# Token order, 2 KB stores, late bias product and a new order of work in a fused window-attention and top-2 expert kernel

## The reference

```
x = x + conv(ln_c(x))             # window attention on channel-normalised x
t = tokens(x)                     # (4, 16384, 64)
t = t + ffn(ln_t(t))              # top-2 of 8 experts
x = from_tokens(t)

conv: qkv = xh @ w_qkv.T;  windows of 8 x 8 tokens, 4 heads of 16
      attn = softmax(q k^T * 0.25 + bias[rel_index]);  out = (attn v) @ w_proj.T + b_proj
ffn:  p = softmax(x @ router_w + router_b);  top_p, top_i = top_k(p, 2);  top_p /= sum(top_p)
      out = sum over the two of top_p * (x @ expert_w[top_i] + expert_b[top_i])
```

## Time and profile before

| | |
|---|---|
| median of 3 runs | 1326.42 us (1312.49 to 1327.78) |
| profiled execution, own time | 1318.76 us |
| its span, first to last instruction | 1316.9 us |
| mean granted TensorE clock in it | 0.93 of full speed |
| busy share: TensorE, VectorE, ScalarE, GpSimd | 85%, 71%, 57%, 32% |
| DMA queues' share of 16 engines | 64.0% (the program's own queue) |
| DMA packets, and those under 512 B | 143202, 81984 |

### The profile page before, as it was taken

One profiled execution on the slowest core, in us unless ns is written; L12 is line 12 of the kernel. 1 busy time (PEld: TensorE's weight loads), 2 busy tenths in 40 slices (PEclk: granted clock), 3 DMA queues, 4 the chain that ended last, 5 costly groups with the idle time before them and its releaser, 6 DMA issues.

```text
span 1316.9 us, 40785 instructions
## 1 busy us (share of the span) xinstructions
PE 1124.7 (85%) x16486; PEld 600.8 (46%) x16486; DVE 938.3 (71%) x1431; ACT 753.4 (57%) x1185; POOL 417.4 (32%) x359
## 2 busy tenths in 40 slices
PE   3687998998899879988998989999899999988853
PEld 2344554445455434444444445455444544544411
DVE  3346778788777867777688777777767678778742
ACT  1366656566666655665566656666555566665410
POOL 1002233233332332333233233332333333323342
PEclk9988889898998988999899989998888899998877
DMA  4013567777666678766567875666678667656777
GB/s 158 1 29 87 138 156 183 183 177 172 145 166 147 166 166 189 165 155 154 130 164 179 189 188 139 161 162 153 152 182 189 154 162 171 159 136 141 170 174 166
DMA packets 143202, 202.75 MB, mean 154 GB/s; under 512 B 81984, under 2 KB 94656, under 8 KB 142912
## 3 DMA queue, kind: packets, MB, share of 16 engines
q1 hardware_dynamic: 143040, 200.28, 64.0%
HBM read 160.37 MB, written 23.07 MB: 139 GB/s over the span
## 4 chain that ended last, share of the span: by engine, by line
PE 37%; issue 23%; DMA 13%; POOL 10%; SPq 6%; DVE 5%; ACT 4%; POOLq 0%; ACTq 0%; DVEq 0%
DMA gz<-gates_dram 11%; PE bank L593 8%; POOL gz L903 6%; PE bank L476 6%; PE bank L509 5%; SPq L320 4%; PE bank L437 3%; PE bank L491 3%; PE bank L526 3%; POOL tt L877 2%; PE bank L533 2%; DMA gates_dram<-gsb 2%; SPq L312 2%; PE bank L464 2%; PE bank L428 1%
## 5 line engine op out<-in xcount | busy, mean ns | idle before, releaser
L1021 DVE TENSOR_TENSOR gz<-gz,tt 128x1024 f32<-128x1024 f32 x160 | 242.2, 1515 | 156.7 <-DMA gz<-gates_dram 156.7
L903 POOL TENSOR_TENSOR gz<-gz,tt 128x1024 f32<-128x1024 f32 x96 | 229.5, 2391 | 224.4 <-DMA gz<-gates_dram 224.4
L593 PE MATMUL bank<-gz,wex 64*64 64x512 f32 x2048 | 259.6, 623 | 26.4 <-issue 24.2
L877 POOL TENSOR_TENSOR tt<-prj,xs 128x512 f32<-128x512 f32 x64 | 103.6, 1639 | 361.9 <-ACT prj L764 361.9
L1000 DVE TENSOR_REDUCE mx<-bank 128x16 f32<-128x1024 f32 x128 | 156.5, 1223 | 71.9 <-PE bank L476 69.1
L476 PE MATMUL bank<-km,qs 32*64 32x128 f32 x4096 | 183.7, 297 | 0.3
L509 PE MATMUL bank<-cst,probs 128*128 128x128 f32 x1024 | 174.6, 296 | 3.2 <-ACT pt L747 3.1
L747 ACT ACTIVATE pt<-bank 128x512 f32<-128x512 f32 x256 | 152.1, 594 | 40.8 <-PE bank L509 37.7
L1007 DVE TENSOR_TENSOR probs<-bank,mx 128x1024 f32<-128x1024 f32 x128 | 156.8, 1225 | 11.5
L476 PEld LDWEIGHTS bank<-km,qs 32*64 32x64 f32 x4096 | 117.7, 140 | 92.9 <-issue 88.8
L740 ACT ACTIVATE probs<-probs 128x1024 f32<-128x1024 f32 x128 | 134.9, 1054 | 17.8 <-DVE probs L1007 17.5
(11 more groups left out here) (100 smaller groups left out, 1447.2 us busy)
## 6 DMA issues: line engine op xcount, KB each, us to landing
gz<-gates_dram SPq DMA_DIRECT2D x512, 256.0 KB, 6.8
xs<-in_x SPq DMA_DIRECT2D x32, 512.0 KB, 6.9
tx<-tt SPq DMA_DIRECT2D x128, 128.0 KB, 2.6
out<-ob SPq DMA_DIRECT2D x128, 128.0 KB, 6.8
gates_dram<-gsb SPq DMA_DIRECT2D x32, 192.0 KB, 2.1
grow<-gates_dram SPq DMA_DIRECT2D x192, 32.0 KB
gz<-in_rel SPq DMA_DIRECT2D x1, 2048.0 KB, 9.0
cst<-in_consts SPq DMA_DIRECT2D x1, 359.0 KB, 3.0
```

The costliest lines, as they stand in the source:

```text
L593: last = mm(bank[64 * x:64 * x + 64, Y_BANK + a, :], wex[64 * a:64 * a + 64, e, :], gz[64 * a:64 * a + 64, e, x * CH:(x + 1) * CH], start= ...
L877: tt_(as_windows(tt[s.buf(4)][:, x, :]), as_windows(prj[:, x, :]), chunk_windows(xs[s.buf(4)], x), op=ALU.add).then_inc(t_ready, 1)
L903: tt_(gz[:, e, :], gz[:, e, :], tt[s.buf(4)][:, :, :].rearrange("p x t -> p (x t)"), op=ALU.mult).then_inc(z_pool, 1)
L1021: tt_(gz[:, e, :], gz[:, e, :], tt[s.buf(4)][:, :, :].rearrange("p x t -> p (x t)"), op=ALU.mult).then_inc(z_dve, 1)
```

## The change

**Tokens in row order.** `tt` and `ob` become plain rows of 1024 tokens in image order. `residual` writes its half through a window view, so the attention's half x now goes to the left or right eight-column groups of each row. `router`, `swap_tokens` and `finish` then cut the row at its middle, that is between image rows 3 and 4 of the strip, and `finish` adds plain rows.

**Stores.** A store's half is four image rows of a channel, one piece of 2 KB; before it was eight pieces of 256 B.

**Bias product last.** `experts` opens the banks with expert 0 (and waits there for the sum of the strip before to be read), `expert_bias_rows` closes them behind expert 7, and `finish` waits for a new semaphore `y_full` set by it.

**One stage number fewer.** `LAST_STAGE` is 6, 38 steps; most calls move one stage down. Ten steps stand ahead of the loop, which keeps five passes of four.

**Another order in all five lists.** SyncE: the wait for `write_gates` moves from `load_gate_rows` into the first `spread_gates`; gates 0 to 6 are loaded right behind the write, gate 7 at the head of the next step, then `store`, then the `grow` pieces, `load`, `swap_tokens`, `write_gates`. VectorE: `scale_x`, `gated` 5 and 6 stand at the head, ahead of `move_logits`. ScalarE: `log_var`, `inverse_std` and `high_std` move from the head to behind `move_pt` 7. TensorE: `spread_std` closes the list, and the router follows four attention calls at its head. GpSimd: second half of `residual` first, first half last. The bank rounds follow: "K" now stands right behind "lgT" (whose reader is VectorE's `move_logits`), and "spread" stands last in both.

```diff
-    LAST_STAGE = 7
+    LAST_STAGE = 6
-    out_parts = out.rearrange("(q a) c (s r) (x k) -> q x a c s r k", a=2, r=WS, x=2)
+    out_parts = out.rearrange("(q a) c (s x r) w -> q x a c s (r w)", a=2, x=2, r=WS // 2)
...
         ROUNDS = {
-            0: [("lgT", 5, L_ready, 2), ("spread", 3, xr_ready, 1), ("K", 3, k_ready, 2), ("Q", 3, q_ready, 1),
-                ("gT", 5, gsb_ready, 1), ("V", 3, v_ready, 2), ("proj", 4, prj_ready, 1), ("stats", 2, var_done, 1)],
-            1: [("router", 5, lg_ready, 1), ("spread", 3, xr_ready, 1), ("K", 3, k_ready, 2),
-                ("Q", 3, q_ready, 1), ("V", 3, v_ready, 2), ("proj", 4, prj_ready, 1)],
+            0: [("lgT", 4, L_ready, 2), ("K", 2, k_ready, 2), ("Q", 2, q_ready, 1), ("stats", 1, var_done, 1),
+                ("gT", 4, gsb_ready, 1), ("V", 2, v_ready, 2), ("proj", 3, prj_ready, 1), ("spread", 1, xr_ready, 1)],
+            1: [("router", 4, lg_ready, 1), ("K", 2, k_ready, 2), ("Q", 2, q_ready, 1), ("V", 2, v_ready, 2),
+                ("proj", 3, prj_ready, 1), ("spread", 1, xr_ready, 1)],
         }
...
             def load_gate_rows(s):
 
-                sp.wait_ge(gates_written, s.count(16, 16))
...
             def spread_gates(s, e):
 
+                if e == 0:
+                    sp.wait_ge(gates_written, s.count(16, 16))
+                    sp.sem_inc(sp_waited, 1)
                 wait(sp, e_done, s.count(E, e + 1, lag=1))
...
             def expert_bias_rows(s):
 
                 pe.wait_ge(grow_loaded, s.count(96, 96))
-                wait(pe, y_ready, s.count(1, 0))
                 for a in range(2):
-                    mm(bank[:, Y_BANK + a, :], eb[:, :], grow[s.buf(2)][:, a, :], start=True, stop=False,
-                       skip_group_check=True)
+                    last = mm(bank[:, Y_BANK + a, :], eb[:, :], grow[s.buf(2)][:, a, :], start=False, stop=True,
+                              skip_group_check=True)
+                last.then_inc(y_full, 1)
...
-                tt_(as_windows(tt[s.buf(4)][:, x, :]), as_windows(prj[:, x, :]),
+                tt_(chunk_windows(tt[s.buf(4)], x), as_windows(prj[:, x, :]),
                     chunk_windows(xs[s.buf(4)], x), op=ALU.add).then_inc(t_ready, 1)
...
-                dve.wait_ge(e_done, s.count(E, E))
+                dve.wait_ge(y_full, s.count(1, 1))
...
-                tt_(ob[s.buf(2)][:, :, :, :].rearrange("p r v k -> p v r k"), as_windows(two_banks(Y_BANK)),
-                    as_windows(tx[:, s.buf(2), :, :].rearrange("p a t -> p (a t)")), op=ALU.add).then_inc(y_ready, 1)
+                tt_(ob[s.buf(2)][:, :], two_banks(Y_BANK), tx[:, s.buf(2), :, :].rearrange("p a t -> p (a t)"),
+                    op=ALU.add).then_inc(y_ready, 1)
```

More of the change, by code:

```diff
@@ new lines, in _ @@
+                if s[4].on:
+                    router(st, s[4])
+                if s[3].on:
+                    values(s[3], 1)
+                    transposes(s[3], 3)
+                if s[4].on:
+                    transpose_logits(st, s[4])
+                if s[5].on:
+                    experts(s[5], 3)
+                if s[2].on:
+                    keys(st, s[2])
+                if s[5].on:
+                    experts(s[5], 4)
+                    experts(s[5], 5)
+                    experts(s[5], 6)
@@ new lines, in _ @@
+                if s[2].on:
+                    queries(st, s[2])
+                if s[5].on:
+                    experts(s[5], 7)
+                if s[3].on:
+                    denominators(s[3], 0)
+                if s[2].on:
+                    scores_left(s[2], 0)
+                if s[3].on:
+                    transposes(s[3], 4)
+                if s[2].on:
+                    scores_right(s[2], 0)
+                if s[1].on:
+                    channel_sums(st, s[1])
+                if s[3].on:
+                    values(s[3], 2)
+                    values(s[3], 3)
+                    transposes(s[3], 5)
+                    denominators(s[3], 1)
@@ new lines, in _ @@
+                if s[4].on:
+                    move_logits(s[4])
+                if s[1].on:
+                    square(s[1])
+                if s[3].on:
+                    move_pt(s[3], 3)
+                if s[4].on:
+                    log_token_var(s[4])
+                    token_std(s[4])
+                if s[2].on:
+                    move_k(s[2], 0)
+                    move_k(s[2], 1)
+                if s[3].on:
+                    exps(s[3], 3)
+                if s[2].on:
+                    move_q(s[2])
@@ L1105, in _ @@
                 s = st.strips()
-                if s[3].on:
-                    variance(s[3])
-                    guard_variance(s[3])
-                if s[7].on:
-                    finish(s[7])
-                if s[6].on:
-                    gated(s[6], 3)
+                if s[2].on:
+                    scale_x(s[2])
+                if s[5].on:
+                    gated(s[5], 5)
+                    gated(s[5], 6)
+                if s[4].on:
+                    move_logits(s[4])
+                    token_statistics(s[4])
@@ new lines, in _ @@
+                if s[3].on:
+                    row_max(s[3], 3)
+                    shift(s[3], 3)
+                if s[4].on:
+                    logits(s[4])
+                    top_one(s[4])
+                    pick_one(s[4])
+                    top_two(s[4])
+                    pick_two(s[4])
+                if s[3].on:
+                    normalise(s[3], 0)
+                if s[4].on:
+                    gates(s[4])
+                if s[2].on:
+                    row_max(s[2], 0)
@@ L1113, in _ @@
+                if s[1].on:
+                    variance(s[1])
+                if s[2].on:
+                    shift(s[2], 0)
+                if s[3].on:
+                    normalise(s[3], 1)
+                if s[1].on:
+                    guard_variance(s[1])
                 if s[5].on:
-                    move_logits(s[5])
+                    finish(s[5])
+                if s[2].on:
+                    row_max(s[2], 1)
                 if s[3].on:
-                    low_part(s[3])
@@ L1117, in _ @@
-                if s[5].on:
-                    token_statistics(s[5])
+                    normalise(s[3], 2)
+                if s[2].on:
+                    shift(s[2], 1)
+                if s[1].on:
+                    low_part(s[1])
                 if s[4].on:
-                    normalise(s[4], 0)
+                    gated(s[4], 0)
                 if s[3].on:
-                    scale_x(s[3])
-                if s[5].on:
-                    logits(s[5])
-                    top_one(s[5])
+                    normalise(s[3], 3)
@@ L1155, in _ @@
-                if s[5].on:
-                    gated(s[5], 2)
+                    gated(s[4], 2)
+                if s[2].on:
+                    shift(s[2], 2)
+                if s[4].on:
+                    gated(s[4], 3)
                 if st.c == 0:
```

311 lines of the change are left out of this document (122 added, 189 removed).

## The result

The changed kernel takes 1374.26 us (median of 4 runs, 1371.29 to 1383.76). The kernel before, run beside it, takes 1327.1 us. The ratio is 1.0387, 95% interval 1.034 to 1.0434: 3.9% slower. The forecast was 1313 and its range ended at 1356. In experiment 10 three of ten executions were slow ones (1332 to 1340 us) and are left out of its time; all other executions given here were fast ones.

What follows compares the result with a forecast made beforehand. Before: bound by TensorE, one stall and the clock; after: by the gate-load loop. Step 35.8 + 1.0 clock + 0.7 returns = 37.5 against 37.9 us, times 29, ends -1: 1306 profiled, 1313 median; range 1262 to 1356.

Steps and rivals of the forecast that it cites:

- the loop through the gate loads: From one ScalarE gate copy over write, gate loads, top-2 to the next: floor of a step, 35.8 us.
- TensorE's way: The loop's path through keys and TensorE's own order: 35.7 us, against 35.0 through VectorE.
- the 2.65 us stall: TensorE's wait before the logit transposes, ScalarE being held in log_var; the change was to remove it.
- layout and ends: Row-order edits costed at nothing; start of the run 0 (bounds -5 and +5), end of the run -1 us.
- 22.3 + 12.3 + 1.1: Gate copy's end to keys, keys to the gate transposes, then to the next gate copy's end: 35.7 us.
- Gate 6 lands at X + 20.6: X is the end of ScalarE's gate copy; 2.1 us to the first load's issue, then 18.5 to landing.
- The statistics at 0.65 us: VectorE's token statistics after gate 6's product, taken as 0.65 us, done 0.1 us before gate 7 lands.
- rival B: GpSimd's gated 7 takes the port first, statistics wait about 2.3 us: step 38.0, 1328 us; chance 0.14.
- The clock at 1.0 us: TensorE's half-clock loss from split gaps, on the stretch after keys: 1.0 us a step, bounds 0 and 3.0.
- The returns: Four issue waits of 6.0 us, 2.4 swallowed, 1.3 added for clock: 0.7 us a step over 29 steps.
- Rival C: Keys stands for gate 6, clock falls each step, 3.0 us in the loop: step 39.5, 1372 us; chance 0.13.
- the mark that was to speak for C (0.93): Sign from TensorE's granted clock: below 0.93 speaks for C, above 0.96 for the clock staying up.
- TensorE's largest wait is before keys: Sign: TensorE waits longest before keys, released by VectorE's copy of the logits; wrong if longest elsewhere.

Runs made afterwards that it cites:

- experiment 10: The changed kernel with U = 8 and VectorE's move_logits and token_statistics ahead of both gated 5 and gated 6: 1317.55 us, ratio 0.9953 to the kernel before.
- Experiment 2: The changed kernel with one wait more: GpSimd's gated 7 waits until token_statistics of the next strip are done: 1339.16 us, ratio 1.0129 to the kernel before.
- experiment 1: The changed kernel with VectorE's move_logits and token_statistics moved ahead of gated 6: 1317.32 us, ratio 0.9957 to the kernel before.
- experiment 4: The changed kernel with the six grow pieces issued on SyncE ahead of the load of gate 0 again: 1422.41 us, ratio 1.0766 to the kernel before.
- experiment 3: The changed kernel with each gate load bringing only the left 512 of 1024 columns: 1245.79 us, ratio 0.9403 to the kernel before.

## Why the prediction was wrong, step by step

**Which step failed.** The forecast was 1313, the time is 1374. The structure held: the loop through the gate loads binds, VectorE waits for gates 5 and 6, keys wait for the logits' bank, TensorE's way is the longer by 0.6 us (0.7 in the forecast), the 2.65 us stall is gone, and layout and ends are worth 0 and 3 us. What failed is what the sum added to the loop: nothing for the port, nothing for a gate write that lands late, and 5 us for a return. Plain steps were forecast at 36.8 (35.8 and 1.0 for the clock) and are 38.25; returns at 5 us each and are 8.8 by the trace, 12 by taking them away. In the profiled execution the steps took 67 us more than the forecast: 25 plain ones 1.5 each, the four with a return 5.2 each, and the last two 7.7 together, which the forecast had left as they were.

The trace parts the 26 plain steps (without the last) by what happened in them. In three neither did a collision hold the statistics nor did the write land late: 36.5 us, the forecast's 36.8 within 0.3. In 13 there was the collision alone: 38.3. In four the late write alone: 38.1. In six both: 39.6. Experiment 2, without the collision, has 36.5 and 38.2 for the first and the third kind. In the plain step shown the forecast's loop of 22.3 + 12.3 + 1.1 is 23.5 + 13.8 + 1.1 = 38.4: from X to keys, from keys to the gates' transposes, and on to the next X. The middle term is 12.0 in nearly all steps of experiment 2, so it was right wherever the port is free.

**"Gate 6 lands at X + 20.6".** It is taken at X + 22.0 (median over 31 steps). Two parts: the loads take about 1.1 us longer (19.6 from the first issue to gate 6, median) than the 18.5 in the last strip of the kernel before, from which the figure came; and in eleven steps the gate write itself lands after 2.7 to 4.1 us instead of 2.1. With the write in time gate 6 is taken at X + 21.8 in the mean, with a late one at X + 23.1. A stretch at the end of the run was a poor stand-in for the middle: in the last strip of experiments 1, 2 and 4 the last load for gate 6 lands 18.6 to 18.7 us after the first issue, 0.6 to 0.8 sooner than the median of the same run. But after the change it took 19.5 in the last strip too, and why stays open.

**The statistics at 0.65 us.** This is rival B, and it came true in 19 of 31 steps beside the forecast's loop. I had seen that the margin was 0.1 us and gave B 0.14. With a margin smaller than the error of either landing time, half would have been right, and its cost belongs in the sum, not beside it: 1.2 us a step in the mean, 1.8 in a step that has it (38.3 against 36.5). I also let B hide up to 1.5 us of clock loss behind it; ScalarE's list hides nothing, since `move_k` waits behind the same statistics and holds the queries, so TensorE's way round grew with VectorE's. Experiment 2 shows 35 us.

**The clock at 1.0 us.** The whole stretch ran at 0.94 as before, so about 2.3 us a step again, but much of it falls into the returns (0.81 to 0.85 in these steps), and little of the rest shows on the loop: nine plain steps at 1.00 took 38.0 us in the mean, the 17 others 38.6. The three steps of 36.5 had gate 6 about 1.1 us later than forecast, so of the 1.0 for the clock little can have been on the loop: two misses of like size cancelled there, which is luck.

**The returns.** The pause was right (6.0 forecast, 6.5 in the mean). I had 2.4 of it swallowed by spare time and 1.3 added for the clock. TensorE's pause falls between spread_std and the router, the logits come late, and everything behind them shifts by it; the half clock after it falls on the same stretch, about 4.8 us lost in the one shown. None of the four steps has a collision at the statistics, and they are 10.6 us over the 36.5 of a step without one: about the pause and the lost clock together, so next to nothing was swallowed.

**Rival C** has the right number, 1372, by another cause. Its 3.0 us of clock a step did not happen. The profiled execution's clock, 0.917, is on the side of the mark that was to speak for C (0.93), but the low part stands in the returns and at the ends, not behind keys: such a mark for the whole run could not tell the two apart. Its case was that a loop which leaves TensorE idle has no slack for anything that adds to it. That much was right, and its chance of 0.13 was far too small: every error in a loop's sum that one can make by leaving something out is of one sign. "TensorE's largest wait is before keys" was wrong as well; in the plain step shown the longest idle is 1.65 at queries, with 1.45 at keys, and over the run the waits for the experts' products lead (59.2 us for VectorE's and 35.2 for GpSimd's).

## What to carry to other kernels

When an edit removes a stall, follow the longest way from one pass to the next through every engine and queue; if that way includes transfers, its sum is the step, and a hair's breadth between two users of one port counts as a collision. Put work that waits for a late transfer behind the work that others wait for: one such move was worth 57 us here. Before a mean step is explained, part the steps by what happened in them: here three kinds differed by 3 us. A loop return costs most where no engine has slack, so try the number of steps in a pass again after each reordering.

## What the runs showed of the hardware

The write of the gates (192 KB) lands 2.1 us after X in most steps and after 2.7 to 4.1 us in eleven of 31. In all eleven a 16 KB packet of the instruction queue started between X + 0.4 and X + 1.1 and took 0.9 to 1.7 us; in none of the other 20 steps did one start there (in one, a packet of 8 KB). In the trace of the kernel before, one write of 31 landed more than 0.5 us late, after 2.9 us, and it is again the only one with such a packet there (X + 0.6). That the packet holds the write back is thus likely; no run moved the packets to try it.

A return to the loop's head leaves TensorE idle for 4.8 to 8.7 us wherever the loads have their full size, with nothing in the profile that it waited for. With half the bytes (experiment 3) the four pauses are 2.6 to 3.2 us, and the return costs that kernel 2.7 us (38.2 against 35.5), against 8.8 with whole loads. So the pause grows with the traffic of the gate loads. In the changed kernel a 16 KB packet of the instruction queue starts 3.1 to 4.7 us into each of the four pauses, with half loads within the first 0.6. That TensorE waits for its instructions behind the loads fits this and was not tried otherwise. With 20 steps written out the longest pause without a named cause was 2.7 us and the longest step 39.3 us.

Two 16-column VectorE operations of 0.18 us took 2.3 us where a GpSimd product held them up; the one shown above started 0.08 us after that product and ended 0.03 us after it. The Trainium skill ("SBUF — State Buffer", section "SBUF: two separate sides") calls it a lock held for the whole instruction; the trace agrees.
